# Sort keys in eleven steps a bit, group parameters copied ahead, step biases loaded in the first stage, ten fillers instead of forty at the head of a mixer

## The reference

```python
x = x + quantised_product(ln(x), ctx)            # 8-bit fake-quantised matmul
x = x + mamba_mixer(ln(x), in_proj, conv, dt, A, D, norm_w, out_proj)
x = x + lora_experts(ln(x), base_W, router, lora_A, lora_B)
x = x + point_cloud(ctx, ln(x), ...)             # windows of neighbours in 4 sort orders
x = x + sparse_linear(ln(x), weight, mask)
x = x + ffn(ln(x), w12, b12, w3, b3)
```

```python
P = Q - 1
for i in range(3):
    cond = X[i] & Q > 0
    t = (X[0] ^ X[i]) & P
    new_X0 = where(cond, X[0] ^ P, X[0] ^ t)
    if i != 0:
        X[i] = where(cond, X[i], X[i] ^ t)
    X[0] = new_X0
```

## Time and profile before

| | |
|---|---|
| time, three executions | 1065.52, 1067.68, 1069.34 us (median 1067.68) |
| profiled execution | 1066.81 us |
| its span in the trace | 1065.2 us |
| TensorE busy (PE) | 1003.7 us, 94% |
| TensorE weight loads (PEld) | 768.2 us, 72% |
| VectorE (DVE) | 754.2 us, 71% |
| ScalarE (ACT) | 455.9 us, 43% |
| GpSimd (POOL) | 438.7 us, 41% |
| mean granted TensorE clock | 0.987 |

### The profile page before, as it was taken

The page is one execution under the profiler, slowest core; times in us unless marked ns, Lnnn a source line. Parts: engine busy times, 40 slices in busy tenths (PEclk is TensorE's granted clock), DMA queues, the critical chain, the costliest instruction groups (busy, mean ns, idle before and its releaser), DMA issues. The chain is left out here.

```text
span 1065.2 us, 38584 instructions
## 1 busy us (share of the span) xinstructions
PE 1003.7 (94%) x16232; PEld 768.2 (72%) x16232; DVE 754.2 (71%) x1898; ACT 455.9 (43%) x701; POOL 438.7 (41%) x408
## 2 busy tenths in 40 slices
PE   4899789999999999999989999989889999998998
PEld 2799777796968879557876777769876666664585
DVE  7598893756648375975678999967578888996310
ACT  6243233241432314212247777752356676662010
POOL 1101263030220202200169999950378888886000
PEclk9999889999999999999999999999999999999999
DMA  8997666878778783864313222224122222221550
GB/s 333 406 387 267 223 248 255 328 285 293 298 244 346 265 325 124 311 240 114 53 27 73 69 67 67 69 62 77 30 50 60 58 57 58 57 61 30 229 246 21
DMA packets 58363, 181.40 MB, mean 170 GB/s; under 512 B 10041, under 2 KB 10793, under 8 KB 57898
## 3 DMA queue, kind: packets, MB, share of 16 engines
q1 hardware_dynamic: 55850, 171.80, 47.3%
q0 software_dynamic: 2432, 8.42, 2.2%
HBM read 150.26 MB, written 0.56 MB: 142 GB/s over the span
## 5 line engine op out<-in xcount | busy, mean ns | idle before, releaser
L535 PEld LDWEIGHTS ps<-hT,ring 128*128 128x128 f32 x2304 | 262.3, 194 | 13.3 <-ACT xc L666 6.8
L535 PE MATMUL ps<-hT,ring 128*128 128x128 f32 x2304 | 264.2, 278 | 6.6 <-ACT xc L666 6.6
L1806 POOL TENSOR_TENSOR X<-sortedT,ring 128x960 f16 (+1 forms) x84 | 156.9, 1867 | 0.0
L937 POOL TENSOR_TENSOR y_y<-y_z,sgate 128x512 f32<-128x512 f32 x16 | 20.0, 1270 | 217.0 <-DVE y_z L872 200.8
L1824 POOL TENSOR_TENSOR S<-S,den 128x480 f32<-128x480 f32 x86 | 86.6, 1007 | 37.9 <-DVE den L1743 37.9
L1831 POOL TENSOR_TENSOR PP<-S,PP 128x480 f16<-128x480 f32 x86 | 97.9, 1138 | 3.5 <-ACT PP L1615 3.5
L571 PE MATMUL ps<-wt,y_n 128*128 128x512 f32 x224 | 99.1, 595 | 0.0
L782 DVE SCALAR_TENSOR_TENSOR xc<-xpad,parg,xc 128x128 f32<-128x128 f32 x192 | 58.3, 366 | 56.4 <-ACT xc L666 55.2
L1519 PE MATMUL ps<-PT,ring 128*64 128x120 f16 x2752 | 96.1, 221 | 2.0 <-DMA PT<-P_turned 1.7
L1615 ACT CAST PP<-S 128x480 f16<-128x480 f32 x86 | 66.9, 778 | 60.9 <-POOL S L1824 54.6
L1519 PEld LDWEIGHTS ps<-PT,ring 128*64 128x64 f16 x2752 | 81.8, 110 | 14.8 <-DMA PT<-P_turned 6.1
(11 more groups left out here) (322 smaller groups left out, 1607.2 us busy)
## 6 DMA issues: line engine op xcount, KB each, us to landing
ring<-in_w_in SPq DMA_DIRECT2D x36, 2048.0 KB, 8.7
wt<-in_w_out SPq DMA_DIRECT2D x14, 2048.0 KB, 7.8
PT<-P_turned SPq DMA_DIRECT2D x344, 64.0 KB
ring<-in_w SPq DMA_DIRECT2D x8, 1024.0 KB, 12.0
ctx_chunks<-in_ctx SPq DMA_DIRECT2D x4, 1024.0 KB, 8.9
ring<-in_ctx SPq DMA_DIRECT2D x4, 1024.0 KB, 16.6
krow<-keys_scratch POOLq DMA_DIRECT2D x8, 512.0 KB, 6.4
mchunk<-in_mask_t POOLq DMA_DIRECT2D x8, 512.0 KB, 8.6
```

The source lines that it names most:

```text
L535: mm = nc.tensor.matmul(ps[:, bank, j * T:(j + 1) * T], weights[:, j, kc * P:(kc + 1) * P], k.hT[:, kc, :], start=kc == 0, stop=kc == KC - 1)
L1806: ins = gp.tensor_tensor(fcopy(c.X[u][:, 0, 0:1], full(cnt)), fcopy(c.fsT[:, 0, bass.ds(it * STEP, 1)], trio(start, cnt, 1)), fcopy(c.fTr[ ...
```

## The change

It has five parts.

- `transform` does a bit in eleven steps: the sign shift of all three axes is one instruction (128 x 96), the mask of axes 1 and 2 one (128 x 64), and the two exclusive-ors of t1 into X0 and into the axis are one on the pair of them (128 x 64, t1 read twice).
- `finish` does its three last exclusive-ors in one instruction (128 x 96).
- `parameters(g)` is taken out of `group`: the copy for group g + 1 stands at the end of group g in the loop, and the copy for group 1 between the transform of bits 3, 2, 1 and `finish`. The semaphores it waits for are those of before.
- `head_par` is loaded by the first stage, ahead of the context chunks, with a semaphore of its own; ScalarE waits for `par` and `parbc` only after the step sizes.
- The mixer's head has 5 fillers (ten records), not 20.

```diff
@@ stage_quantised_product, SyncE
                 sp.dma_start(crow[b * 3 * NT:(b + 1) * 3 * NT, :], ...
+            sp.dma_start(k.head_par[:, :], dr["head_par"]).then_inc(k.head_par_in, 16)
             for c in range(CHUNKS):
@@ class SortKeys
     def transform(self, bits):
-        vec, link = self.nc.vector, self.link
-        X = [self.flat(1, i) for i in range(3)]
-        t1, m = self.w.t1[:, :], self.w.m[:, :]
+        vec, link, w = self.nc.vector, self.link, self.w
+        axes = w.q[:, 1].rearrange("p i v b t -> p i (v b t)")
+        X0, t1 = axes[:, 0, :], w.t1[:, :]
         for bit in bits:
             low = (1 << bit) - 1
-            for i in range(3):
-                link(vec.tensor_scalar(m, X[i], 31 - bit, 31, SHL, SAR))
-                if i == 0:
-                    link(vec.scalar_tensor_tensor(out=X[0], in0=m, scalar=low, in1=X[0], op0=AND, op1=XOR))
-                else:
-                    link(vec.tensor_scalar(m, m, low, None, AND))
-                    link(vec.tensor_tensor(t1, X[0], X[i], XOR))
-                    link(vec.scalar_tensor_tensor(out=t1, in0=m, scalar=low, in1=t1, op0=XOR, op1=AND))
-                    link(vec.tensor_tensor(X[0], X[0], t1, XOR))
-                    link(vec.tensor_tensor(X[i], X[i], t1, XOR))
-                    link(vec.tensor_tensor(X[0], X[0], m, XOR))
+            link(vec.tensor_scalar(w.m[:, :, :], axes, 31 - bit, 31, SHL, SAR))
+            link(vec.scalar_tensor_tensor(out=X0, in0=w.m[:, 0, :], scalar=low, in1=X0, op0=AND, op1=XOR))
+            link(vec.tensor_scalar(w.m[:, 1:3, :], w.m[:, 1:3, :], low, None, AND))
+            for i in (1, 2):
+                pair = axes[:, 0:i + 1:i, :]
+                link(vec.tensor_tensor(t1, X0, axes[:, i, :], XOR))
+                link(vec.scalar_tensor_tensor(out=t1, in0=w.m[:, i, :], scalar=low, in1=t1, op0=XOR, op1=AND))
+                link(vec.tensor_tensor(pair, pair, fcopy(t1, [[0, 2], [1, 32]]), XOR))
+                link(vec.tensor_tensor(X0, X0, w.m[:, i, :], XOR))
@@ finish
-        for i in range(3):
-            link(vec.tensor_tensor(X[i], X[i], t1, XOR))
+        axes = w.q[:, 1].rearrange("p i v b t -> p i (v b t)")
+        link(vec.tensor_tensor(axes, axes, fcopy(t1, [[0, 3], [1, 32]]), XOR))
@@ stage_mixer
-            sp.dma_start(hp[:, :], dr["head_par"]).then_inc(s_par, 16)
...
-            hold_clock(nc, k, 0, 4 * HOLD)
+            hold_clock(nc, k, 0, HOLD)
...
-            act.wait_ge(s_par, 48)
+            act.wait_ge(k.head_par_in, 16)
             nc.scalar.activation(ea[:, :], hp[:, 1:2], ACT.Exp).then_inc(s_dtr, 1)
...
             act.wait_ge(s_const, 7)
+            act.wait_ge(s_par, 32)
@@ VectorE
-            v.wait_ge(s_par, 48)
+            v.wait_ge(s_par, 32)
...
-            def group(g, first, final=False):
-                if not first:
+            def parameters(g):
+
+                if not (isinstance(g, int) and g == 0):
                     v.wait_ge(s_yn, 2 * g)
                 vec.tensor_copy(parg[:, :, :].rearrange("p j c -> p (j c)"), par[:, bass.ds(g, 1), :].rearrange("p a c -> p (a c)")).then_inc(s_pg, 1)
+
+            def group(g, first, final=False):
                 v.wait_ge(s_pg, g + 1)
...
                 if not first and not final:
                     after_out(g - 1)
+                    parameters(g + 1)
+
+            parameters(0)
             group(0, True)
             keys.transform(range(BITS - 7, 0, -1))
+            parameters(1)
             keys.finish()
```

More of the change, by code:

```diff
@@ L296, in _ @@
             hold_clock(nc, k, 0, 2 * HOLD)
-KEY_STEPS = 10 + 5 + (BITS - 1) * (2 + 2 * 7) + 2 + 8 + 8 + 2 + 2 + 1
+KEY_STEPS = 10 + 5 + (BITS - 1) * (3 + 2 * 4) + 2 + 6 + 8 + 2 + 2 + 1
 SHL, SAR, SHR = ALU.logical_shift_left, ALU.arith_shift_right, ALU.logical_shift_right
@@ L373, in finish @@
         X = [self.flat(1, i) for i in range(3)]
-        t1, m = w.t1[:, :], w.m[:, :]
+        t1, m = w.t1[:, :], w.m[:, 0, :]
         for i in (1, 2):
@@ L425, in stage_mixer @@
         parbc = sb("parbc", [P, 2 * NG, CK + 1])
-        hp, ea = sb("head_par", [P, 2]), sb("exp_A", [P, 1])
+        hp, ea = k.head_par, sb("exp_A", [P, 1])
         dtr, dta, dte, dts, dtp, dtq = (sb(f"dt_{i}", [P, T]) for i in "raespq")
@@ L439, in stage_mixer @@
         w.q = sb("w_q", [P, 2, 3, 2, B, NT], I32)
-        w.t1, w.m = sb("w_t1", [P, 32], I32), sb("w_m", [P, 32], I32)
+        w.t1, w.m = sb("w_t1", [P, 32], I32), sb("w_m", [P, 3, 32], I32)
         w.spread, w.key = sb("w_spread", [P, 192], I32), sb("w_key", [P, 64], I32)
@@ L1963, in build @@
         k.coord = k.sb("coord", [P, B * 3 * NT], F32)
+        k.head_par = k.sb("head_par", [P, 2], F32)
         k.keys = k.sb("keys", [P, NM * B * NT], F32)
@@ L1969, in build @@
         k.moe_in = k.sem("moe_in")
-        k.coord_ready = k.sem("coord_ready")
+        k.coord_ready, k.head_par_in = k.sem("coord_ready"), k.sem("head_par_in")
         k.ps = ctx.enter_context(nc.psum_tensor("ps", [P, 8, HALF], F32))
```

## The result

Fifteen executions of the changed kernel have a median of 1060.76 us (1056.47 to 1063.73), against 1068.85 us for fifteen of the kernel before (1064.84 to 1070.81). The ratio is 0.9927, 95% interval 0.9913 to 0.9942: 7.8 us faster (6.2 to 9.3 by the interval), where the sum of the prediction had 11.64 and the forecast was 1055.6. The profiled execution took 1057.7 for a span of 1056.1; it is one of the quicker ones, so its own gain of 9.1 us flatters the change.

The account below looks back on a forecast made before the run. TensorE, busy nearly all the span, was taken as the bound, so other engines' edits pay only where it waits; 6.60 + 2.30 + 0.24 + 2.95 - 0.45 = 11.64 us gave a forecast of 1055.6 us, range 1052 to 1059.5.

Parts of the forecast that it names:

- The stop ahead of block 2: Group 1's projections, TensorE waiting for the parameter copy: stop goes entirely, 6.60 us, and the clock fall behind it, 2.30.
- the copy ahead alone: Group 1's parameter copy before `finish`: this edit alone takes nearly the whole 6.60 us stop, releasing block 0 at about 129.5.
- What comes next after it: Group 1's ranks and xs after the stop: from 4.0 us of room to 0.2 of loss; no loss taken.
- rival C: Ranks late in group 1, or step biases' load dearer than taken: together up to 2 us, 1056 to 1057.6; chance 0.08.
- Eleven steps: VectorE's key transform: a bit costs 2.56 us instead of 3.55, 1.0 us a bit saved over nine bits.
- The second place: TensorE's wait for xs of group 0: 0.73 us instead of 0.97, 0.24 gained from shorter steps.
- Cover for the copy more than a gain of its own: VectorE's shorter key steps: mainly slack for group 1's parameter copy, which comes 2.8 us ahead of TensorE.
- reading of the long steps: VectorE key steps beside GpSimd: two-input instructions from SBUF contend with GpSimd's reads; 4.5 us of stretching kept.
- Fewer fillers: Mixer's head, ten filler records instead of forty: first projection starts at 41.25 instead of 44.20, 2.95 us gained.
- Step biases in the first stage: head_par's load ahead of the context chunks: about 0.45 us lost, bounds 0 and 1.0; no gain from the earlier biases.
- rival B: Mixer's head: the clock falls as thirty fillers go, 1057.5 to 1059.0 us; chance 0.30.
- Rival D: The clock fall at 110 disappears too, as the wait before it is shorter: 1052.2 to 1053.7 us; chance 0.08.

Follow-up runs that it names:

- experiment 4: Copy of group 1's parameters ahead of `finish`, alone, on the kernel before: 1062.64 us, ratio 0.9959.
- experiment 1: Changed kernel with the ranks of group 1 moved behind xs of that group: 1052.86 us, ratio 0.9864.
- experiment 7: Changed kernel with GpSimd's point cloud constants moved behind the gate product of group 1: 1059.88 us, ratio 0.9931.
- experiment 2: Kernel before with the ranks of group 1 moved behind xs, nothing else: 1068.45 us, ratio 0.9999.
- experiment 6: Version of experiment 1 with sixteen steps a bit again: 1058.26 us, ratio 0.9901.
- experiment 8: Forty filler records again: in the changed kernel 1062.23 us, ratio 0.9957; in the version of experiment 1 1058.48 us, ratio 0.99.
- experiment 9: Kernel before with ten filler records at the mixer's head, nothing else: 1067.73 us, ratio 1.0009.
- experiment 10: Changed kernel with the load of head_par back in the mixer, behind par and parbc: 1061.67 us, ratio 0.996.
- experiment 5: Kernel before with eleven steps a bit and the shorter `finish`, nothing else: 1063.76 us, ratio 0.9962.
- experiment 11: Version of experiment 1 with group 1's ranks at that group's very end, behind the copy for group 2: 1054.01 us, ratio 0.9866.
- experiment 3: Changed kernel with the parameter copy of group 1 back behind `finish`: 1059.55 us, ratio 0.9934.

## Why the prediction was wrong, point by point

**The stop ahead of block 2 (6.60 + 2.30).** Right as a mechanism and in size: 0.33 left, full clock behind it. The last three bits took 12.14 us (109.54 to 121.68) where the prediction had 12.2. The claim that the copy ahead alone takes nearly the whole stop held too (1.08 left in experiment 4).

**What comes next after it: the step that failed.** The prediction took "4.0 of room to 0.2 of loss; I take no loss" for the ranks, and priced the rival (C) at two microseconds at most with a chance of 0.08. It measured 4.88 us of stop and 1.4 us of low clock behind it (158.10 to 162.20, against 152.92 to 155.58 in experiment 1), 6.3 together; experiment 1 gives back 6.7, or 5.2 by its trace, with the 1.11 that come back in group 2 taken off. Idle time of xs in group 1 is the sign that the prediction itself had given for rival C. Its terms:
- TensorE's need was put at 158.6 in the old clock, which is about 155.9 after the gain at the head. It was 152.94. The difference of 2.9 is the fall of the clock at 110 (1.90 in the block and 0.89 in the decay sums, 1.98 against 1.09), which I had kept in as part of TensorE's time. In that execution it did not come. This part of the stop is no loss against the sum, which kept the fall: it is a further gain of 2.9, given back at once.
- VectorE's end of xs was put at 158.8 at the latest, 156.1 in the new clock. It was 157.58. The bound was the old distance from keys to ranks, 12.3 us, and that distance grew to 14.4 (127.64 to 142.04). All of the growth is in the store, which took 5.98 us to the issue of the row load instead of 3.89; the row of constants behind it is 8.03 in both. The prediction laid the old distance to the store and load of the key row and did not see the constants. The row load itself became longer, too, 7.5 us from issue to landing instead of 4.4, with a DMA share of 1.04 from 134 to 142 where it had been 0.50 from 138 to 145; experiment 7 shows that this was hidden under the constants, with 0.9 us to spare. Why the store took longer stays open. The weight loads of the now uninterrupted projections are an obvious candidate, but no run took them away, and the mean share does not settle it: the store took 3.85 and 3.87 us in experiments 2 and 6 at a share of 0.04, 3.89 in the kernel before at 0.57, and 5.98 at 0.65.
- The clock fall behind a new stop, 1.4 us, was priced nowhere, though the prediction had just priced one behind the old stop.
- So against the sum it is about 3.4 us: products at 157.82 instead of 155.9, and 1.4 of low clock. In the two traces the projections of group 2 start at 170.38 and 162.20, 8.2 us apart. The measured gain of 7.8 is 3.8 under the sum.
- The range reached down to 1052 for a cheap surprise and up to 1059.5. The measured median is 1.3 above it.

**Eleven steps (1.0 us a bit).** Right: 2.56 us. The second place, xs of group 0, gave 0.09 (0.97 to 0.88) where the sum had 0.24. "Cover for the copy more than a gain of its own" was half right. On the kernel before they are worth 4.1, in the version of experiment 1 4.0, and both places named in the prediction show it. What it missed is that the sixteen steps did not quite fit once the head was shorter. One reading of the long steps was too simple as well: the longest beside GpSimd's work has one input, not two.

```profile
119.39 1.82 DVE L360 TENSOR_SCALAR w_m<-w_q 128x32 int32<-128x32 int32 x1
```

**Fewer fillers (2.95).** Right: 2.84 in the trace, 3.2 and 3.8 us by the two runs of experiment 8. But only together with the early biases: alone they gave nothing (experiment 9). The prediction called the biases' own gain 0 as "conv waited for nothing TensorE needed"; it overlooked the bank that ScalarE empties at `dt_r`, whose wait was hidden by 1.2 us under the fillers. In the sum it did no harm, since both parts were in the change.

**Step biases in the first stage (-0.45).** Wrong by its whole size: no loss shows. SyncE issued the first context load 0.39 us later (4.50 against 4.11), and the last chunk was at ScalarE 0.13 us earlier. Other traces agree: 27.47 in experiment 7 with the early load, 27.80 and 27.58 in experiments 10 and 9 without it. The issue of these loads was not what bound them.

**The clock at the head (rival B, 0.30).** Did not happen in any of the eight traces with ten records: the granted clock is 1.00 from 36 to 48 in each, and in the changed kernel the first projection takes 2.05 us, as with forty records. **Rival D** (the fall at 110 goes) did happen in the profiled execution, and in those of experiments 1, 5, 7, 8, 10 and 11, while in 2, 3, 4, 6 and 9 the clock fell at 110 as before. The reason that the prediction gave, a shorter wait ahead of it, does not decide it: TensorE waited 0.88 for xs in experiments 1 and 3, and the clock fell in 3 alone. In the profiled execution it bought nothing, as the chain was next in line.

## What to carry to other kernels

When a stop goes, ask of each later wait of the same engine how much room it had, not whether it waited: room is the difference between when the operand was ready and when the engine came for it, and every gain ahead, the intended ones and those of the clock, is taken from it. A chain through DRAM need not keep its length when it moves: from keys to ranks it was 12.3 us before and 14.4 after. Price the clock behind a new stop as well as behind the old one. And before a large stop is attacked, write down which other chain the engine needs next; here moving 14 us of ranks behind the instruction that TensorE needed was worth 6.7 us with the change, which alone gave 7.8, and nothing without it.

## What the runs showed of the hardware that was not expected

- An 8-element copy on VectorE lasted 6.36 us in the changed kernel, from 135.65 to 142.01, and ended with GpSimd's iota (140.97 + 1.01), behind a row of memsets without a gap. With the memsets moved away it took 0.17. In the kernel before the same copy lasted 2.41 and ended with the iota as well, and so it did in experiments 3, 4, 5, 8 (in the changed kernel), 9 and 10, with 2.40 to 5.93 us by when it started, each time within 0.04 us of the iota's end. It was held for the rest of the row, not for one of its instructions. The Trainium skill (SBUF — State Buffer, "Who interferes with whom") has a VectorE copy among the operations that can contend with GpSimd for the shared ports; the trace agrees, and shows that it can lose several times in a row.
- The maximum over partitions on GpSimd (L951 after, L946 before) began at 46.7 to 47.5 in all fourteen traces, whether its input was ready at 44.4 (before), 44.2 (experiment 8) or 41.5 (after). VectorE waited 2.86 for it in the first and 5.99 in the last. Its start does not follow its input there. In every trace it comes 5.8 to 6.7 us after GpSimd's instruction before it, and the profile shows nothing that it waits for in between; what fills that time no run shows. So the head of the key chain did not move with the fillers.
